# Two exchanged coefficient tables: turned on TensorE for eight channels, copied by DMA for the other 120

## The reference

```python
# x: (64 batches, 128 channels, 2048 steps); one length per batch
dt = exp(log_dt);  A = -exp(log_A_real) + 1j * A_imag;  dtA = A * dt      # 128 channels x 64 modes
Cs = (C[..., 0] + 1j * C[..., 1]) * (exp(dtA) - 1) / A
K = 2 * einsum('hn,hnl->hl', Cs, exp(dtA[:, :, None] * arange(2048))).real
u = x * mask                                   # steps below the batch's length
y = irfft(rfft(u, 4096) * rfft(K, 4096))[..., :2048] + u * D[:, None]
out = x + y * mask
```

## Time and profile before

| | us |
|---|---|
| median of 3 runs (lowest, highest) | 852.72 (852.28, 853.17) |
| the profiled execution, its own time | 853.14 |
| its span in the profile | 851.3 |
| PE busy in the span | 816.7 (96%) |
| DVE, ACT, POOL busy | 730.0, 619.2, 641.3 |
| start of `k_fenced` on TensorE | 42.28 |
| start of the first Toeplitz matmul of channel 0 | 51.41 |

### The profile page before, as it was taken

How to read it: one execution, slowest core, us unless ns; L and a number is a source line. 1 busy time by engine, 2 the same in 40 slices (tenths; PEclk the granted TensorE clock), 3 DMA queues, 4 the chain that set the end, 5 groups by cost and what they waited for, 6 DMA issues and landing times.

```text
span 851.3 us, 22217 instructions
## 1 busy us (share of the span) xinstructions
PE 816.7 (96%) x6168; PEld 752.9 (88%) x6168; DVE 730.0 (86%) x2020; ACT 619.2 (73%) x1717; POOL 641.3 (75%) x708
## 2 busy tenths in 40 slices
PE   0799999999999999999999999999999999999997
PEld 0779998989999999999998999999999999999996
DVE  7878988888888888888888888888888888888886
ACT  4777776777777777777777777777777777777774
POOL 5887776777777878787787878777787877778771
PEclk9999999999999999999999999999999999999999
DMA  5235877777777787777877777777777877777875
GB/s 108 50 74 145 197 189 183 192 186 184 190 187 199 185 193 192 185 197 184 196 185 193 191 186 197 184 195 185 194 191 190 196 184 195 185 194 189 197 191 137
DMA packets 161391, 152.69 MB, mean 179 GB/s; under 512 B 13656, under 2 KB 161240, under 8 KB 161240
## 3 DMA queue, kind: packets, MB, share of 16 engines
q1 hardware_dynamic: 161064, 152.15, 72.5%
q10 hardware_dynamic: 304, 0.26, 0.1%
HBM read 84.02 MB, written 67.30 MB: 178 GB/s over the span
## 4 chain that ended last, share of the span: by engine, by line
PE 89%; DVE 4%; DMA 3%; ACT 1%; SPq 1%; issue 1%; DVEq 0%
PE y L1021 13%; PE y L1023 13%; PE y L1022 13%; PE y L1067 13%; PE v L1038 11%; PE xt_even L1006 6%; PE xt_odd L1006 6%; PE v L1021 3%; PE v L1022 3%; DMA xall<-in_x_dram 3%; PE v L1023 3%; PE y L1016 2%; PE y L1017 2%; SPq L355 1%; ACT room L542 0%
## 5 line engine op out<-in xcount | busy, mean ns | idle before, releaser
L542 ACT ACTIVATE room<-v 64x192 f32<-64x192 f32 (+1 forms) x768 | 235.8, 307 | 171.9 <-DVE v L911 156.0
L911 DVE SCALAR_TENSOR_TENSOR v<-v,RV,mid 128x192 f32<-128x192 f32 (+2 forms) x512 | 192.3, 376 | 55.0
L911 DVE SCALAR_TENSOR_TENSOR mid<-room,RV,v 128x192 f32<-128x192 f32 (+2 forms) x512 | 184.3, 360 | 42.1 <-ACT room L542 23.5
L1021 PE MATMUL y<-thi,uhi 128*128 128x256 f32 x511 | 186.0, 364 | 0.0
L900 DVE COPY_PREDICATED xall<-mask,y 128x512 f32<-128x512 int32 x254 | 174.4, 735 | 1.7 <-issue 1.7
L1021 PE MATMUL y<-fhi,zhi 128*128 128x256 f32 x511 | 154.3, 302 | 1.3 <-DVE zlo L735 1.2
L1023 PE MATMUL y<-thi,ulo 128*128 128x256 f32 x511 | 144.2, 282 | 0.0
L1023 PE MATMUL y<-fhi,zlo 128*128 128x256 f32 x511 | 143.8, 281 | 0.0
L1022 PE MATMUL y<-tlo,uhi 128*128 128x256 f32 x511 | 143.7, 281 | 0.0
L1022 PE MATMUL y<-flo,zhi 128*128 128x256 f32 x511 | 143.7, 281 | 0.0
L521 POOL TENSOR_TENSOR room<-W,B 128x512 f32 (+1 forms) x127 | 141.7, 1116 | 0.0
(11 more groups left out here) (195 smaller groups left out, 1939.6 us busy)
## 6 DMA issues: line engine op xcount, KB each, us to landing
xall<-in_x_dram SPq DMA_DIRECT2D x256, 256.0 KB, 4.6
out_dram<-xall SPq DMA_DIRECT2D x254, 256.0 KB, 3.4
traw<-krows SPq DMA_DIRECT2D x128, 128.0 KB, 3.0
NXY<-B SPq DMA_DIRECT2D x2, 512.0 KB, 6.2
krows<-ksb SPq DMA_DIRECT2D x8, 1.0 KB, 2.2
krows<-ksb SPq DMA_DIRECT2D x8, 4.0 KB, 3.6
krows<-ksb SPq DMA_DIRECT2D x8, 11.0 KB, 4.0
out_dram<-xall SPq DMA_DIRECT2D x1, 128.0 KB, 2.5
```

The source lines that it names most:

```text
L542: return act.activation(dst, src, ACT.Copy)
L911: return dve.scalar_tensor_tensor(out=out, in0=src, scalar=RV[:, k:k + 1, h], in1=other, op0=ALU.mult, op1=ALU.add)
L1021: pe.matmul(o, a_hi, b_hi, start=start, stop=False, skip_group_check=True)
```

## The change

X2 and Y2 are turned only for channels 0 to 7: the transpose takes 8 partitions of the source instead of 128, eight powers in one step, in the 64 columns of a bank. For channels 8 to 127 SP copies W1's partition halves crosswise into W2, four DMAs of 64 partitions by 7680 bytes (`swap`), in slots 0 and 1 of the loop; POOL waits for them (s_swap) before channel 8. W2 is laid out like W1. The exchange by itself can't change a sign for one half only, so the sign moves: X2 has none now, Y2 has the other one, B2 has one in place of it, and E is a sum where it was a difference, so that POOL's last instruction becomes two of 128x256, and `turn_e` waits only for the first of them (s_pe). The steps go from 26 to 22, of which three are DVE's as against four. X and Y of powers 12 to 15 are not doubled any more, the doubling of 8 to 15 is one instruction of 1024 elements, and one doubling of NB moves from POOL to ACT. There are three groups of `keep_warm` (12, 16, 8) in other places in lieu of one (16).

```diff
-         ("B1", 12), ("B2", 12), ("X1", 12), ("X2", 12), ("Y1", 12), ("Y2", 12),
-         ("B1", 8), ("B2", 8), ("X1", 8), ("X2", 8), ("Y1", 8), ("Y2", 8),
...
+         ("B1", 12), ("B2", 12), ("X1", 12), ("Y1", 12),
+         ("B1", 8), ("B2", 8), ("X1", 8), ("Y1", 8), ("X2", 8), ("Y2", 8),
...
+SIGN = {("R", 1): 1, "Y1": 0, "Y2": 1, "B2": 1}
+BY_VECTOR = [STEPS.index(k) for k in [("B1", 4), ("B2", 4), ("X1", 4)]]
+WARM, WARM_Y, WARM_B = 12, 16, 8
...
+            def swap(w, half):
+                to, by = (slice(half * N, half * N + N) for half in (half, 1 - half))
+                sp.dma_start(W2[to, w, EARLY:, :], W1[by, w, EARLY:, :]).then_inc(s_swap, 16)
...
                     load_t(*on(g, j, 2))
+                if start and j < 2:
+                    for half in range(2):
+                        swap(j, half)
...
-            pool.tensor_copy(NB[:, late, 0, :], NB[:, late, 1, :]).then_inc(s_blate, 1)
...
+                if isinstance(g, int) and h == EARLY:
+                    pool.wait_ge(s_swap, 16 * 4)
...
-                pool.tensor_tensor(pf[k][:], tw1[:].rearrange("p a b c -> p a (b c)"),
-                                   tw2[:].rearrange("p a b c -> p a (b c)"), ALU.subtract).then_inc(s_pf, 1)
+                pool.tensor_tensor(pf[k][:, 0], e[0], e[1], ALU.add).then_inc(s_pe, 1)
+                pool.tensor_tensor(pf[k][:, 1], f[0], f[1], ALU.subtract).then_inc(s_pf, 1)
...
+                    n = EARLY if name in SWAPPED else P
...
+                        mm = pe.transpose(dst, source(t, r)[0:n].rearrange("p c n -> p (c n)"), ident[0:n, 0:n])
```

More of the change, by code:

```diff
@@ L196, in s4d_kernel @@
         s_gpa = sem("s_gpa")
+        s_swap = sem("s_swap")
+        s_pe = sem("s_pe")
         s_yini = sem("s_yini")
@@ L528, in channel @@
                 pool.wait_ge(s_gpa, 2 * h)
-                pool.tensor_tensor(pf[k][:], tw1[:].rearrange("p a b c -> p a (b c)"),
-                                   tw2[:].rearrange("p a b c -> p a (b c)"), ALU.subtract).then_inc(s_pf, 1)
+                e, f = (tuple(t[:, a].rearrange("p b c -> p (b c)") for t in (tw1, tw2)) for a in range(2))
+                pool.tensor_tensor(pf[k][:, 0], e[0], e[1], ALU.add).then_inc(s_pe, 1)
+                pool.tensor_tensor(pf[k][:, 1], f[0], f[1], ALU.subtract).then_inc(s_pf, 1)
                 if exists(g, j, -2) and exists(g, j, -3):
@@ L604, in _ @@
             take(("R", 0), ("R", 1))
-            both = slice(0, 2)
             act.wait_ge(s_nb, 1)
             double_b(slice(12, 16))
-            act.wait_ge(s_nxy, 1)
-            double_xy(slice(12, 16), both)
             take(("B1", 12), ("B2", 12))
-            take(("X1", 12), ("X1", 12))
+            take(("X1", 12), ("Y1", 12))
             act.wait_ge(s_nb, 2)
             double_b(slice(8, 12))
-            take(("X2", 12), ("Y2", 12))
             act.wait_ge(s_nxy, 2)
-            double_xy(slice(8, 12), both)
-            take(("B1", 8), ("Y1", 8))
+            double_xy(slice(8, 16), slice(0, 2))
+            take(("B1", 8), ("Y2", 8))
             act.wait_ge(s_nxy, 3)
             double_xy(slice(0, SQ // 2), 1)
-            take(("Y2", 8), ("B1", 4))
+            take(("Y1", 0), ("Y2", 0))
+            act.wait_ge(s_nb, 3)
+            copy(NB[:, 0:SQ // 2, 0, :], NB[:, 0:SQ // 2, 1, :]).then_inc(s_bdup, 1)
+            take(("B1", 0), ("B2", 4))
             for t in range(STEPS.index(("B1", 0)), STEPS.index(("B2", 4)) + 1):
@@ L625, in _ @@
             copy(b0[:, 1], B2[:, 0, :]).then_inc(s_b0, 1)
-            take(("X1", 0), ("X1", 4))
+            take(("X1", 0), ("X2", 0))
             act.wait_ge(s_kfill, 1)
@@ L883, in first_table @@
             def first_table(n):
-                w1, w2 = (w.unsqueeze(2).broadcast_to(square) for w in (W1[:, n, 0, :], W2[:, n, :, 0]))
+                w1, w2 = (w[:, n, 0, :].unsqueeze(2).broadcast_to(square) for w in (W1, W2))
                 b1, b2 = (b0[:, w].unsqueeze(1).broadcast_to(square) for w in range(2))
@@ L993, in _, with keep_warm @@
             pe.wait_ge(s_pool0, 1)
-            def keep_warm(n, bank):
+            def keep_warm(n, t):
+                if t >= BANKS:
+                    pe.wait_ge(s_free[t % BANKS], t // BANKS)
                 for _ in range(n):
-                    pe.transpose(bank[:, 0:P], ident[:], ident[:])
+                    pe.transpose(pro[t % BANKS][:, 0:P], ident[:], ident[:])
             def turn_x(g, j, par):
@@ L1126, in turn @@
                         pe.wait_ge(s_free[t % BANKS], t // BANKS)
-                    for r in range(3 if STEPS[t][0] == "R" else 4):
-                        dst = pro[t % BANKS][:, r * P:(r + 1) * P]
-                        if STEPS[t][0] in ROWS:
+                    name = STEPS[t][0]
+                    n = EARLY if name in SWAPPED else P
+                    for r in range({"R": 3, "X2": SQ // 2, "Y2": SQ // 2}.get(name, 4)):
+                        if name == "R":
+                            dst = pro[t % BANKS][:, r * P:(r + 1) * P]
+                        elif name in SWAPPED:
+                            dst = pro[t % BANKS][:, r:EARLY * SQ // 2:SQ // 2]
+                        else:
                             dst = pro[t % BANKS][:, r:512:4]
-                        mm = pe.transpose(dst, source(t, r).rearrange("p c n -> p (c n)"), ident[:])
+                        mm = pe.transpose(dst, source(t, r)[0:n].rearrange("p c n -> p (c n)"), ident[0:n, 0:n])
                     mm.then_inc(s_fill[t % BANKS], 1)
```

59 lines of the change are left out of this document (32 added, 27 removed), and 2 rows, old and new, of the table STEPS.

## The result

| | before | changed |
|---|---|---|
| median, us (lowest to highest) | 853.06 (851.06 to 857.12) | 855.84 (853.76 to 858.32) |
| executions | 21 | 21 |
| ratio, 95% interval | | 1.003 [1.0019, 1.0041] |
| the profiled execution, its own time | 853.14 | 857.05 |
| its span | 851.3 | 854.1 |

The forecast was 852.4, with a range that ended at 854.6. By the ratio the change is slower by 2.6 us, and its median lies above the whole range.

What follows compares the result with a forecast made beforehand. It took TensorE's matmuls to bound the loop and ACT's copies out of PSUM the prologue's end; -0.3 us in the prologue and 0 in the loop gave 852.8 profiled, 852.4 for the median, range 850.2 to 854.6.

Steps and rivals of the forecast that it cites:

- 13 or 14 are slow if the clock rises at 30.0 as before: Prologue, TensorE: of the first 16 transposes from 27.07, 13 or 14 run at the lower clock; done at 30.4.
- TensorE's queue as the bound: Rival, prologue: clock rises at 32.6, small transposes cost 0.11, TensorE never waits for ACT; ulo 1.9 late, 854.6; chance 0.10.
- Late clock alone is +0.9: Prologue: the clock's late rise without dear small transposes costs +0.9 us, inside 0.2%.
- The early clock: Rival, prologue: clock rises before 27.1, first 16 transposes cost 1.75 not 3.3; time 850.2 to 851.1; chance 0.25.
- `k_fenced` from 42.28: End of the prologue: `k_fenced`, with the turned x of channel 0, moves from 42.28 to 42.05.
- For ulo: DVE's instruction on which the loop starts: uhi at 43.8, ulo 0.55 behind, 44.35 against 44.65, a gain of 0.3 us.
- The small transposes: Prologue, TensorE: 32 transposes of 8 partitions at 0.07 each, ends 0.03 and 0.11, about 1 us either way.
- the fillers: Prologue, TensorE: transposes without a reader; twelve until 31.7, 16 from 34.6 to 36.3, 8 from 37.7 to 38.6.
- the twelve outlasting ACT's second doubling of NB at 31.6: Prologue: the point from which TensorE's queue becomes the bound; the forecast itself had the twelve done at 31.7.
- transposes don't raise the clock: Fourth rival, prologue: by a page's rule transposes stay at 0.213 each, ending at 53, 11 us late; 863; chance 0.01.
- POOL's split: Loop: subtraction in two pieces costs about 0.15 more per slot, hidden under 1.17 + 0.23 us of idle time; nothing.
- x of channel 6: Loop: its loads wait behind the swaps, 1 to 2 us of cover, cost nothing; DMA rival 855 to 856, chance 0.06.

Runs made afterwards that it cites:

- the three profiles of the changed prologue: Profiles of the changed kernel (855.84), of it without the four swap DMAs (855.37), and of it with POOL's subtraction joined in one piece (854.89).
- the kernel without sixteen and eight: Changed kernel without the groups of 16 and 8 filler transposes, the twelve kept and nothing added ahead: 854.80, ratio 1.0022.
- the experiment without its sixteen: Kernel before without its 16 transposes of the identity ahead of B1, so that TensorE has the changed kernel's gap: 853.33, ratio 0.9998.
- twice as many parts: Kernel before with POOL's subtraction in four pieces of 128x128: 852.88, ratio 0.9992.
- the kernel with six ahead: Changed kernel with six identity transposes ahead of B1, filling the gap, and the groups of 12, 16 and 8 kept: 855.45, ratio 1.0023.
- the kernel without both: Changed kernel without the groups of 16 and 8; two such runs: nothing added, 854.80 (ratio 1.0022), or six transposes ahead, 852.04 (0.9989).
- the two others that have the very same prologue: Changed kernel without the four swap DMAs, 855.37 (ratio 1.0029), and changed kernel with POOL's subtraction joined again, 854.89 (1.0021).
- both give 2.9: Changed kernel with six identity transposes ahead of B1 and without the groups of 16 and 8: 852.04, ratio 0.9989.
- five profiles with before's prologue: Kernel before, plus its versions with copies alone (ratio 1.0004), two-part subtraction (1.0018), four-part subtraction (0.9992), and itself rerun unchanged (0.9997).

## Why the prediction was wrong

**The step that failed** is "13 or 14 are slow if the clock rises at 30.0 as before". It rose at 31.8, 32.4 and 32.9 in the three profiles of the changed prologue. The cause is the gap of 1.19 us from 25.9 to 27.1, where before had put its sixteen transposes. Over all sixteen profiles the two groups don't touch: with TensorE busy after the rotations the rise lies between 27.3 and 30.0 (eleven), with the gap between 30.5 and 32.9 (five, the kernel without sixteen and eight the earliest). The prediction had this mechanism among its rivals (32.6, TensorE's queue as the bound) at 0.10, and did not see that it was likelier than "as before", which assumed that a gap changes nothing. It priced it at "Late clock alone is +0.9". The first two profiles have +0.97 for `k_fenced`, 42.28 to 43.25, but that agreement is luck: they hold the latest rise before (30.0) and the earliest of the three after, and the means differ by 1.85. The early clock, at 0.25 the largest rival, is in no profile: none has the rise before 27.1.

**Its second fault is the base.** The forecast moved `k_fenced` from 42.28, one execution. Over five it is 41.67. Of the difference between +1.85 measured and -0.23 forecast, 0.61 is that (42.28 - 41.67) and 1.47 the changed kernel's own miss (43.52 - 42.05): 2.4 us of the lower level from 30.0 to 32.4, during which a transpose costs 0.213 instead of 0.109, are 1.2 of it. From B1 to `k_fenced` it took 3.36 where the forecast had 3.15. For ulo the forecast took 0.55 behind uhi; it is 0.63 in both profiles, before (44.02 to 44.65) and after (44.98 to 45.61).

**The small transposes and the fillers** were priced right: small ones 0.068 (forecast 0.07), 16 fillers 1.8 us (forecast 1.7), 8 fillers 0.9 (forecast 0.9) and a wait of 0.25, and ACT waits for the fill of Y1 as described, 1.50 (forecast 36.9 - 35.7 = 1.2). The prediction also saw that the sixteen stand in front of a step whose source is long ready. But as far as Y1 the path is now TensorE's alone and has no slack: what the clock loses there comes out at the end, where in the kernel before it vanishes in ACT's queue (the experiment without its sixteen). The text named this condition, the twelve outlasting ACT's second doubling of NB at 31.6, and that is what happened: they ended at 32.48.

**The rules of the Trainium skill.** The Trainium skill, "TensorE: Matmul & The Clock Gate", section "LDWEIGHTS (loading the stationary operand)", would have made the small ones as dear as the full ones; the trace disagrees, 0.068 against 0.109. The same page of the Trainium skill, "Part 4: PE-mode transpose", by which transposes don't raise the clock, is refuted by the timeline of TensorE after the change: after a stretch of nothing but transposes they go from 0.213 to 0.109 each.

**The loop** came out nearly as forecast. POOL's split is hidden (1.11 us of idle time left, and twice as many parts show nothing). The swaps are hidden but for 0.26 us in slot 3 of one profile out of two, and not where I looked: I had guarded x of channel 6, but it was `traw` in the very slot of the copies that was late. The pair landed in 6.2, as the earlier trace rows had it.

**What stays open.** The 0.4 us outside the span appear with the sixteen and eight (2.20, and 2.15 in the kernel with six ahead) and not in the kernel without both (1.81). They lie outside the profile, where no trace reaches, and 1.90 and 1.99 in the two others that have the very same prologue make the link weak. The kernel with six ahead and all fillers is about 1 us longer than its prologue says; its profile has that time at the end of the kernel, without a cause. And clock and fillers don't add up in the mean spans, each against before on the same chip: either taken away alone gives 0.7, both give 2.9. For the fillers the trace shows why (the second spell at the lower level); for the six ahead it does not.

No kernel here beats the one before: the best ratio of one that computes the reference, 0.9989, has 1 inside its interval.

## What to carry to other kernels

Before forecasting a reordering, find which engine has no idle time in that stretch, and ask who will have none afterwards: work taken from ACT gains nothing if it lets TensorE's fillers, or a slow clock, onto the path. Fillers belong where they fill an idle time that is there anyway (the eight: free, and with them the clock seldom fell), not in front of a step whose source is long ready (the sixteen). Where the stake is a microsecond, take the base from several profiles of the same prologue, and double a suspected cost before believing one interval that barely excludes nothing.

## What was not expected of the hardware

The moment at which the clock rose moved between executions of the same instructions: 27.7, 27.9, 28.9, 29.4 and 30.0 in five profiles with before's prologue, and 2.3 us of the lower level are worth 1.1 us where TensorE is the bound. An idle time of 1.19 us behind a busy spell was followed by the lower level in one profile (37.87) and not in three others (36.76, 36.45 and 36.51), in kernels that differ by six transposes ten microseconds earlier. A transpose of 8 partitions into 8 columns costs 0.068 us, 62% of a full one.
